# A graph network and two attention passes: start with x by columns, bias as a 129th column, and part of each chunk's chain given to ScalarE

## The chip, the cores and the metric

The kernel runs on one core of one Trainium2 chip. The metric is the device time of one execution in microseconds, the median of several runs. TensorE, VectorE, ScalarE, GpSimd and SyncE are the core's engines; the profile calls them PE, DVE, ACT, POOL and SP.

## The reference

N = 4096 rows, F = 128 columns, all in float32. `adj` is 4096 x 4096, row-normalised.

```python
h = maximum(layernorm(x), 0)
# graph layer, hyperbolic; log0(y) = arctanh(|y|) y/|y|, exp0(v) = tanh(|v|) v/|v|
g = h_add(exp0(log0(h) @ embed), embed_bias)
neigh = exp0(adj @ log0(g))
out = exp0(log0(concat(h, neigh)) @ layer)
x = x + h_add(out, layer_bias)
# h_add(a, y): xy = a.y, a2 = a.a, y2 = y.y
#   ((1 + 2 xy + y2) a + (1 - a2) y) / (1 + 2 xy + a2 y2)
h = maximum(layernorm(x), 0)
# two passes: masked softmax over the cosine of rows, times rows, leaky relu
for beta in (beta1, beta2):
    xn = h / |h|
    h = leaky(softmax(where(adj > 0, beta * xn @ xn.T, -1e9)) @ h)
x = x + h
```

## The kernel before

The work falls into three stages.

**The start.** SyncE loads x in four quarters (L323), then the first eight tiles of the transposed adjacency (L331). VectorE takes mean and variance of each of the 32 row blocks (L1191, L1195), the inverse root (`inv_sqrt`, L1127) and normalises block by block (L1204). TensorE transposes the blocks (`h_transposes`, L413), ScalarE applies relu on the way out of PSUM (L782), TensorE multiplies with `embed` (L427) and with the vector `web` = embed . bias (L433), and ScalarE takes squares and a copy of each product (`g_out`, L763). VectorE sums the squares of h itself (L1215). When all eight products are copied (`g_copied`), TensorE multiplies h with the first half of `layer` (L441), and ScalarE copies that out (`h1_out`, L772). VectorE meanwhile works through small 128x32 operations: `norm` (L1136), `product_scalars` (L1164), `norm`, `atanh_over` (L1145), with a tanh and logarithms that ScalarE does on request, and then makes v, the right side of the aggregation, block by block (L1245). TensorE does ten warm-up matmuls (L481) and waits for v's blocks.

**The aggregation.** For each of eight chunks of 512 columns (`aggregate`, L459) TensorE sums 32 float32 matmuls of 128x512 over tiles in a ring that SyncE refills as tiles are used. After the first four matmuls of chunk c+1 it does the layer product of chunk c: four transposes (L448) and four products with `w2` (L450), which need ScalarE's copy `at_sb` of the aggregated sums (L813). Two accumulators alternate. After the fourth tile it transposes the normalised rows t3 of the chunk before (L456, waits for `xn_ready`). ScalarE squares the rows for their lengths (`row_lengths`, L799). VectorE then works through the chunk's chain (`gnn_chunk`, L1267): norm of the lengths, a request for tanh (L1276), t1 = product * scale + h1 (L1283), squares (L1288), products with the layer bias `lb` (L1293), norms, arctanh, scalars, the bias scaled (L1305), the sum (L1308), x added (L1311), layer norm (L1314 to L1331), high and low float16 part into `src` (L1334, L1336) and t3 (L1342). Each engine takes its instructions strictly in the order written, and requests to ScalarE go over the semaphores `asked` and `told`, counted per chunk (`ASKS_CHUNK`). ScalarE's last work in a chunk is a copy of the new x to x_sb (L822); next it waits for the following aggregation and copies it:

```python
act.wait_ge(agg_tiles, c * NT + NT)                                   # L808
nc.scalar.activation(at_sb, acc_ps[:, parity, :], ACT.Copy).then_inc(at_ready, 1)   # L813
```

**The pairs.** The two attention passes go over pairs of 512-row chunks in 144 half steps, software-pipelined in numbered slots: scores on TensorE (L622), exponential (L990) and high halves (L1000) on ScalarE, low halves (L1647) and masks (L1655, L1665) on VectorE, transposes of mirrored blocks (L608) and the weighted sums (L648 to L675) on TensorE. The chain of chunk 7 is woven in: `last_chunk` of ScalarE (L864) and of VectorE (L1423) are the same steps cut at twelve pauses, and at each pause one slot of the pairs runs. Before its first product TensorE needs at_sb of chunk 7 (L499, ScalarE's L870), then t3 of chunk 6 (L503).

Of the kernel before, what the change touches and what calls it, by code (L numbers as in the profile page):

```python
# [26 lines left out]
def build(nc, x, adj, adj_t, embed, layer, embed_bias, layer_bias, beta1, beta2, out):  # L27
# [33 lines left out]
    WARM = 10  # L61

    ctx = ExitStack()
    with ctx:
# [17 lines left out]
        h1_sb = set1[:, NB * F:2 * NB * F].rearrange("p (b f) -> p b f", f=F)  # L82
# [19 lines left out]
        scr_a = work[:, 0:NB * F].rearrange("p (b f) -> p b f", f=F)  # L102
# [10 lines left out]
        at_sb = accs[:, :, :].rearrange("p b w -> p (b w)")[:, 0:CH]  # L113
        unused = accs[:, :, :].rearrange("p b w -> p (b w)")[:, CH:2 * CH].rearrange("p (b f) -> p b f", f=F)

        w1 = sb("w1", [F, 2 * F])
        w2 = sb("w2", [F, F])
# [22 lines left out]
        web = sb("web", [F, 1])  # L140
        ones_h = sb("ones_h", [P, P], f16)
        small = sb("small", [P, 16, NB])
        lengths = small[:, 11, NB // 2:NB // 2 + CB]
        hh = sb("hh", [P, NB])
# [11 lines left out]
        g_ps = [s_ps[:, i, 0:CH].rearrange("p (b f) -> p b f", f=F) for i in range(2)]  # L156
        h1_ps = [s_ps[:, i // 2, ts(i % 2, CH)].rearrange("p (b f) -> p b f", f=F) for i in range(4)]
        gb_ps = acc_ps[:, 0, 0:NB]
        w_ps = s_ps[:, 0, 0:CH].rearrange("p (b f) -> p b f", f=F)
        xt_ps = s_ps[:, 1, 0:CH]  # L160
        ht_ps = [acc_ps[:, 2 + i, :] for i in range(2)]
        rows_ps = s_ps[:, 0, CH:2 * CH].rearrange("p (b f) -> p b f", f=F)
        rows_last_ps = acc_ps[:, 2, :].rearrange("p (b f) -> p b f", f=F)


        w_last_ps = acc_ps[:, 3, :].rearrange("p (b f) -> p b f", f=F)
# [12 lines left out]
        x_in = [sem(f"x_in{i}") for i in range(XP)]  # L179
        embed_in = sem("embed_in")  # L180
# [9 lines left out]
        xs_ready = sem("xs_ready")  # L190
# [4 lines left out]
        gb_done = sem("gb_done")  # L195
# [8 lines left out]
        lengths_made = sem("lengths_made")  # L204
        xn_ready = [sem(f"xn_ready{i}") for i in range(2)]
# [51 lines left out]
        adj_v = adj.rearrange("(b p) j -> b p j", p=P)  # L257

# [56 lines left out]
        ASKS_CHUNK = 5  # L315
# [5 lines left out]
        def _(sp):  # L321
            for i in range(XP):
                sp.dma_start(x_sb[:, ts(i, NB // XP), :], x_v[:, ts(i, NB // XP), :]).then_inc(x_in[i], 16)  # L323
# [84 lines left out]
        def _(pe):  # L408
            pe.wait_ge(consts_made, 6)
            pe.wait_ge(embed_in, 16 * 2)  # L410


            def h_transposes(r):  # L413
                pe.wait_ge(xs_ready, r + 1)
                wait(pe, ht_copied, r - 1)
                for b in range(CB):
                    last = nc.tensor.transpose(ht_ps[r % 2][:, ts(b, P)], scr_b[:, r * CB + b, :], ident[:, :])
                last.then_inc(ht_done, 1)

            h_transposes(0)  # L420
            for r in range(NC):
                if r + 1 < NC:
                    h_transposes(r + 1)
                pe.wait_ge(ht_copied, r + 1)
                wait(pe, g_copied, r - 1)
                for b in range(CB):
                    last = nc.tensor.matmul(g_ps[r % 2][:, b, :], ht_sb[:, ts(r * CB + b, P)], w1[:, 0:F],  # L427
                                            start=True, stop=True)
                last.then_inc(g_done, 1)
                if r == 0:  # L430
                    pe.wait_ge(web_made, 1)
                for b in blocks(r):
                    last = nc.tensor.matmul(gb_ps[:, b:b + 1], ht_sb[:, ts(b, P)], web[:, :], start=True, stop=True)  # L433
                last.then_inc(gb_done, 1)
# [1377 lines left out]
```

## Time and profile before

| | us |
|---|---|
| median of three runs (lowest, highest) | 976.91 (976.67, 977.71) |
| the profiled execution | 978.14 |
| its span, first to last instruction | 976.6 |
| TensorE busy | 929.2 (95%) |
| VectorE busy | 818.8 (84%) |
| ScalarE busy | 511.2 (52%) |
| mean granted clock of TensorE | 0.989 |

A time of a row is counted from the start of the span. L numbers are lines of the kernel before. A float32 matmul stands as two records in the trace. Busy time of an engine is no proof that it sets the end; the rows further down show who waits for whom.

### The profile page before, as it was taken

The numbers are of one execution on the slowest core, as the hardware profiler recorded it, in microseconds if no ns is written. First come the engines' busy times: TensorE is split into PE (matmuls) and PEld (weight loads), VectorE is DVE, ScalarE is ACT, GpSimd is POOL, SyncE is SP. The second block draws the span as 40 slices with busy tenths as digits, with TensorE's granted clock in tenths as the row PEclk, the third lists the DMA queues.
The fourth block names the chain that finished last, engine by engine and source line by source line (L and its number), as shares of the span: only waits on it lengthen the run. The fifth ranks groups of instructions, "written<-read, shape, count | busy, mean of one in ns | idle before, by whom it ended". The sixth has DMA issues, their size and how long they took to land.

```text
span 976.6 us, 22955 instructions
## 1 busy us (share of the span) xinstructions
PE 929.2 (95%) x9012; PEld 695.3 (71%) x9012; DVE 818.8 (84%) x2110; ACT 511.2 (52%) x756; POOL 8.0 (1%) x21
## 2 busy tenths in 40 slices
PE   2989999999996999999999999999999999999996
PEld 2944444444444878888888888778888888888885
DVE  7891888888889987888989898998778887888887
ACT  1711122212126685766656667787565565656564
POOL 0000000000000000000000000000000000000000
PEclk9899999999998999999999999999999999999999
DMA  8338988888861445565465555545565655665630
GB/s 301 143 118 285 307 285 287 277 295 283 301 229 44 174 173 207 196 246 212 179 235 192 222 217 193 180 167 217 197 217 198 246 197 204 221 232 189 246 142 36
DMA packets 29971, 207.26 MB, mean 212 GB/s; under 512 B 3632, under 2 KB 4272, under 8 KB 5296
## 3 DMA queue, kind: packets, MB, share of 16 engines
q1 hardware_dynamic: 28224, 203.44, 57.6%
q0 software_dynamic: 640, 2.10, 0.5%
q8 instruction: 71, 1.16, 0.5%
q10 hardware_dynamic: 1008, 0.33, 0.1%
q14 instruction: 28, 0.23, 0.1%
HBM read 203.75 MB, written 2.10 MB: 211 GB/s over the span
## 4 chain that ended last, share of the span: by engine, by line
PE 69%; DVE 22%; issue 5%; ACT 3%; DMA 1%; DVEq 0%; POOL 0%; SPq 0%; POOLq 0%
PE s_ps L622 17%; PE s_ps L608 10%; PE acc_ps L469 6%; PE acc_ps L675 6%; PE acc_ps L671 6%; PE acc_ps L673 6%; PE acc_ps L652 5%; PE acc_ps L648 5%; PE acc_ps L650 5%; DVE small L1132 1%; DVE small L1134 1%; DVE small L1133 1%; DVE work L1647 1%; ACT work L990 1%; PE s_ps L427 1%
## 5 line engine op out<-in xcount | busy, mean ns | idle before, releaser
L990 ACT ACTIVATE work<-s_ps,beta_bias,beta_scale 128x1024 f32<-128x1024 f32 x144 | 173.4, 1204 | 217.0 <-PE s_ps L622 216.9
L469 PE MATMUL acc_ps<-ring,set 128*128 128x512 f32 x512 | 223.8, 596 | 3.2 <-DVE set L1245 3.2
L1665 DVE SCALAR_TENSOR_TENSOR h_all<-ring,s_ps 128x1024 f32<-128x1024 f32 x112 | 136.7, 1221 | 65.5 <-PE s_ps L608 64.3
L469 PEld LDWEIGHTS acc_ps<-ring,set 128*128 128x128 f32 x512 | 96.8, 191 | 120.3 <-issue 117.6
L1647 DVE TENSOR_TENSOR work<-work 128x1024 f16<-128x1024 f32 x96 | 132.5, 1380 | 5.4 <-ACT work L1000 5.4
L1000 ACT ACTIVATE work<-work 128x1024 f16<-128x1024 f32 x96 | 131.5, 1369 | 3.2 <-DVE work L1655 0.2
L1655 DVE SCALAR_TENSOR_TENSOR work<-ring,work 128x1024 f32<-128x1024 f32 x96 | 116.8, 1217 | 0.0
L622 PE MATMUL s_ps<-xt 128*128 128x512 f16 x432 | 106.4, 382 | 3.8 <-ACT work L990 3.0
L622 PE MATMUL s_ps<-set 128*128 128x512 f16 x432 | 105.0, 379 | 0.5 <-ACT work L990 0.5
L671 PE MATMUL acc_ps<-set,work 128*128 128x129 f16 x576 | 102.4, 219 | 2.7 <-DVE accs L1682 2.7
L671 PE MATMUL acc_ps<-src,work 128*128 128x129 f16 x576 | 103.5, 220 | 1.4 <-DVE work L1655 1.4
L675 PE MATMUL acc_ps<-src,work 128*128 128x129 f16 x576 | 103.9, 224 | 0.0
L673 PE MATMUL acc_ps<-src,work 128*128 128x128 f16 x576 | 103.6, 221 | 0.0
L675 PE MATMUL acc_ps<-set,work 128*128 128x129 f16 x576 | 102.7, 222 | 0.0
L673 PE MATMUL acc_ps<-set,work 128*128 128x128 f16 x576 | 102.5, 219 | 0.0
L652 PE MATMUL acc_ps<-set,h_all 128*128 128x129 f16 x448 | 79.8, 222 | 0.0
L652 PE MATMUL acc_ps<-src,h_all 128*128 128x129 f16 x448 | 79.8, 222 | 0.0
L650 PE MATMUL acc_ps<-src,h_all 128*128 128x128 f16 x448 | 79.6, 219 | 0.0
L650 PE MATMUL acc_ps<-set,h_all 128*128 128x128 f16 x448 | 79.6, 219 | 0.0
L648 PE MATMUL acc_ps<-src,h_all 128*128 128x129 f16 x448 | 79.6, 219 | 0.0
L648 PE MATMUL acc_ps<-set,h_all 128*128 128x129 f16 x448 | 79.6, 219 | 0.0
L608 PE MATMUL s_ps<-ident,work 128*128 128x128 f32 x560 | 73.6, 274 | 3.0 <-DVE work L1647 3.0
(260 smaller groups left out, 1723.2 us busy)
## 6 DMA issues: line engine op xcount, KB each, us to landing
ring<-in_adj_t SPq DMA_DIRECT2D x192, 1024.0 KB, 5.0
x_sb<-in_x SPq DMA_DIRECT2D x4, 512.0 KB, 7.2
out<-x_sb POOLq DMA_DIRECT2D x8, 256.0 KB, 2.8
w<-in_layer ACTq DMA_DIRECT2D x2, 64.0 KB, 8.1
w<-in_embed ACTq DMA_DIRECT2D x1, 64.0 KB, 4.2
eb<-in_embed_bias ACTq DMA_DIRECT2D x1, 64.0 KB, 6.9
lb<-in_layer_bias ACTq DMA_DIRECT2D x1, 64.0 KB, 7.9
beta<-in_beta ACTq DMA_DIRECT2D x2, 0.5 KB, 7.2
```

The lines of the kernel that those rows point to most:

```text
L469: last = nc.tensor.matmul(agg, v_sb[:, jb, :], ring[:, k, b, :], start=jb == 0, stop=jb == NB - 1)
L608: ins = nc.tensor.transpose(turn_ps[:, ib, ts(u, P)], words[x.n % WR][:, ds(u * CH + ib * P, P)], ident[:, :])
L622: last = nc.tensor.matmul(score_ps[:, ts(u, CH)], xt[x.la][:, p, ds(x.b * CH + (x.h * HB + u) * P, P)], xt[x.la][:, q, ds(x.a * CH, CH)], ...
L648: nc.tensor.matmul(mir_ps[:, x.h, o], w[:, WORD_HI, col], src[x.la][:, q, F:AW], start=ib == 0, stop=False)
L650: nc.tensor.matmul(mir_ps[:, x.h, ds(u * PW, F)], w[:, WORD_HI, col], src[x.la][:, q, 0:F], start=False, stop=False)
L652: last = nc.tensor.matmul(mir_ps[:, x.h, o], w[:, WORD_LO, col], src[x.la][:, q, F:AW], start=False, stop=ib == CB - 1)
L671: nc.tensor.matmul(own_ps[:, ib // 2, ds(ib % 2 * PW, PW)], w[:, WORD_HI, col], src[x.la][:, q, F:AW], start=opens, stop=False, skip_group ...
L673: nc.tensor.matmul(own_ps[:, ib // 2, ds(ib % 2 * PW, F)], w[:, WORD_HI, col], src[x.la][:, q, 0:F], start=False, stop=False, skip_group_c ...
L675: last = nc.tensor.matmul(own_ps[:, ib // 2, ds(ib % 2 * PW, PW)], w[:, WORD_LO, col], src[x.la][:, q, F:AW], start=False, stop=False, ski ...
L990: nc.scalar.activation(values[x.n % VR], score_ps, ACT.Exp, bias=beta_bias[:, x.la:x.la + 1], scale=beta_scale[:, x.la:x.la + 1]).then_inc ...
L1647: V.tensor_tensor(w[:, WORD_LO, :], values[x.n % VR], w[:, WORD_HI, :], ALU.subtract)\
L1665: V.scalar_tensor_tensor(turned[x.off % MR].rearrange("p (b j) -> p b j", b=CB), ring[:, x.mir_tile % AR, :, ds(x.h * HB * P, HB * P)], 0. ...
```

## The change

Three groups of edits.

The start: x is also passed transposed (x_t) and loaded by columns, in turns with x (each 512 KB). TensorE centres the columns by a matmul with I - 1/F and needs no normalised rows; ScalarE applies relu and also squares the result; TensorE sums the squares with a column of ones (`h_lengths`); the inverse deviations `ext` come in afterwards as scalars, and as the scale of h1 when ScalarE copies it out, block by block. `web` becomes the 129th column of w1, so L433 goes. VectorE's 32 normalisations and 32 squares go. Four early warm-up matmuls, and 30 instead of 10 before the aggregation, which wait for a semaphore `closing`. Three of the eight h1 copies stand ahead of ScalarE's tanh, four more ahead of the logarithms.

The chunk: w2 . lb and layer . lb are 129th columns of the weights, so the product with the bias comes out of TensorE and costs VectorE two operations on four elements per row. x is added while t1 is scaled, the scaled bias in a second round. The request for tanh is the norm's last step. The high part of `src` is ScalarE's, on request once t2 is scaled, and so is t3, which waits for the scale (`scaled`); both stand at the end of ScalarE's turn. The low part is made by VectorE in the next chunk, behind its request for tanh.

The last chunk: the same, with one step fewer; pauses 2 and 9 move into the middle of `inv_sqrt`. PSUM places of the products change.

```diff
@@ build @@
-    WARM = 10
+    WARM = 30
+    EARLY_WARM = 4
-        w1 = sb("w1", [F, 2 * F])
-        w2 = sb("w2", [F, F])
+        w1 = sb("w1", [F, 2 * PW])
+        web = w1[:, F:F + 1]
+        w2 = sb("w2", [F, PW])
-    ASKS_CHUNK = 5
+    ASKS_CHUNK = 6
@@ sync @@
+            x_columns(0)
             for i in range(XP):
-                sp.dma_start(x_sb[:, ts(i, NB // XP), :], x_v[:, ts(i, NB // XP), :]).then_inc(x_in[i], 16)
+                if i + 1 < XP:
+                    x_columns(i + 1)
+                x_rows(i)
@@ tensor @@
+            def h_columns(r):
+                if r % 2 == 0:
+                    pe.wait_ge(xt_in[r // 2], 16)
+                wait(pe, ht_copied, r - 2)
+                nc.tensor.matmul(ht_ps[r % 3], centre, xt_in_sb[:, ts(r, CH)], start=True, stop=True)\
+                    .then_inc(ht_done, 1)
+            def h_lengths(r):
+                pe.wait_ge(ht_squared, r + 1)
+                for b in blocks(r):
+                    last = nc.tensor.matmul(hh_ps[:, b:b + 1], sq_sb[:, ts(b, P)], ones[:, 0:1], start=True, stop=True)
+                last.then_inc(hh_done, 1)
+            h_columns(0)
+            h_columns(1)
             for r in range(NC):
+                if r + 2 < NC:
+                    h_columns(r + 2)
+                h_lengths(r)
+                if r % 2:
+                    products(r // 2)
+            for r in range(NC // 2, NC):
+                products(r)
...
+            pe.wait_ge(closing, 1)
             for _ in range(WARM):
...
             aggregate(0, 0, False, False)
+            pe.wait_ge(h1_copied, NC)
             aggregate(1, 1, True, False)
@@ scalar @@
             def h1_out(r):
...
-                nc.scalar.activation(h1_sb[:, ts(r, CB), :], h1_ps[r % 4], ACT.Copy).then_inc(h1_copied, 1)
+                for b in range(CB):
+                    q = r * CB + b
+                    last = nc.scalar.activation(h1_sb[:, q, :], part(h1_ps[r % 3], b, PW), ACT.Copy,
+                                                scale=ext[:, q:q + 1])
+                last.then_inc(h1_copied, 1)
+            h_out(0)
             for r in range(NC):
+                if r + 1 < NC:
+                    h_out(r + 1)
+                h_squares(r)
+                if r % 2:
+                    g_out(r // 2)
+            for r in range(NC // 2, NC - 1):
+                g_out(r)
             log_terms(sm(4, NB), sm(5, NB), sm(6, NB))
             g_out(NC - 1)
+            for r in range(0, 3):
+                h1_out(r)
             on(ACT.Tanh, sm(5, NB), sm(4, NB))
...
@@ scalar, gnn_chunk @@
                 on(ACT.Copy, x_sb[:, ds(c * CB, CB), :], t1[:, :, :])
+                on(ACT.Copy, src[0][:, ds(c * CB, CB), F:2 * F], t2[:, :, :], scale=FS)
+                act.wait_ge(scaled, c + 1)
+                for b in range(CB):
+                    last = nc.scalar.activation(t3[:, b, :], t2[:, b, :], ACT.Copy, scale=chunk_scale[:, b:b + 1])
+                last.then_inc(xn_ready[0], 1)
@@ vector, start @@
-            for r in range(NC):
-                for b in blocks(r):
-                    ins = V.tensor_scalar(scr_b[:, b, :], x_sb[:, b, :], mean_var[:, b, 0:1], small[:, 1, b:b + 1],
-                                          ALU.subtract, ALU.mult)
-                ins.then_inc(xs_ready, 1)
...
-            for b in range(NB):
-                ins = V.scalar_tensor_tensor(v_sb[:, b, :], scr_b[:, b, :], 0.0, scr_b[:, b, :],
-                                             ALU.max, ALU.mult, accum_out=hh[:, b:b + 1])
+            step(V.tensor_tensor(sm(3, NB), ext[:, :], ext[:, :], ALU.mult))
+            dve.wait_ge(hh_done, NC)
+            ins = V.tensor_tensor(hh[:, :], hh_ps, sm(3, NB), ALU.mult)
...
+            V.tensor_tensor(rr, xy, xy, ALU.mult).then_inc(closing, 1)
@@ vector, gnn_chunk @@
-                norm(sm(4, CB), sm(1, CB), lengths, EPS, CB)
-                ask(V.tensor_copy(sm(4, CB), sm(4, CB)))
+                norm(sm(4, CB), sm(1, CB), lengths, EPS, CB, ask)
+                if not first:
+                    dve.wait_ge(told, answers[0])
+                    low_part(c - 1)
...
+                V.tensor_tensor(in_pairs(sm(9, CB)), bias_column(w_in), in_pairs(sm(3, CB)), ALU.mult)
...
+                V.tensor_tensor(sm(9, CB), sm(9, CB), h1_sb[:, rows, F], ALU.add)
...
-                for b in range(CB):
-                    ins = V.scalar_tensor_tensor(t2[:, b, :], t1[:, b, :], 1.0, lb[:, :], ALU.mult, ALU.mult,
-                                                 accum_out=small[:, 9, b:b + 1])
-                step(ins)
...
                 for b in range(CB):
-                    ins = V.tensor_scalar(t2[:, b, :], lb[:, :], small[:, 13, b:b + 1], None, ALU.mult)
+                    ins = V.scalar_tensor_tensor(t1[:, b, :], t1[:, b, :], small[:, 12, b:b + 1],
+                                                 x_sb[:, c * CB + b, :], ALU.mult, ALU.add)
                 step(ins)
                 for b in range(CB):
-                    ins = V.scalar_tensor_tensor(t1[:, b, :], t1[:, b, :], small[:, 12, b:b + 1], t2[:, b, :],
+                    ins = V.scalar_tensor_tensor(t1[:, b, :], lb[:, :], small[:, 13, b:b + 1], t1[:, b, :],
                                                  ALU.mult, ALU.add)
-                step(ins)
-                ask(V.tensor_tensor(t1[:, :, :], x_sb[:, rows, :], t1[:, :, :], ALU.add))
+                ask(ins)
...
-                step(V.tensor_scalar(src[0][:, rows, F:2 * F], t2[:, :, :], FS, None, ALU.mult))
                 answered()
-                step(V.scalar_tensor_tensor(src[0][:, rows, 0:F], t2[:, :, :], FS, src[0][:, rows, F:2 * F],
-                                            ALU.mult, ALU.subtract))
+                ask(ins)
                 step(V.tensor_tensor(sm(0, CB), sm(0, CB), sm(1, CB), ALU.mult))
                 step(V.tensor_scalar(sm(0, CB), sm(0, CB), NORM_EPS, None, ALU.max))
                 step(V.reciprocal(sm(1, CB), sm(0, CB)))
-                for b in range(CB):
-                    ins = V.tensor_scalar(t3[:, b, :], t2[:, b, :], small[:, 1, b:b + 1], FS, ALU.mult, ALU.mult)
-                ins.then_inc(xn_ready[0], 1)
+                V.tensor_scalar(chunk_scale, sm(1, CB), FS, None, ALU.mult).then_inc(scaled, 1)
```

## Rows read from the trace of the kernel before

**Rows 1.** Windows: length, busy PE, PEld, DVE, ACT, POOL, granted clock, DMA share, GB/s

```profile
32.00:34.00 2.00, 2.00 (x21) 2.00 (x20) 1.88 (x17) 1.94 (x11) 0.00 (x0) 1.00 0.34 131
...
42.00:44.00 2.00, 2.00 (x11) 2.00 (x11) 1.71 (x9) 0.76 (x1) 0.00 (x0) 0.50 0.00 0
...
184.00:212.00 28.00, 28.00 (x79) 13.30 (x78) 24.44 (x139) 5.96 (x16) 0.00 (x0) 1.00 0.84 295
...
296.00:310.00 14.00, 7.04 (x41) 4.25 (x42) 13.01 (x47) 9.20 (x16) 0.00 (x0) 0.78 0.01 1
```

**Rows 2.** Timeline, two layer products and chain starts: start, duration, instruction

```profile
177.36 0.60 PE L448 MATMUL s_ps<-ident,accs 128*128 128x128 f32 x4
...
180.63 0.17 DVE L1139 TENSOR_SCALAR small<-small 128x4 f32<-128x4 f32 x1
...
206.59 0.60 PE L448 MATMUL s_ps<-ident,accs 128*128 128x128 f32 x4
...
210.10 0.16 DVE L1139 TENSOR_SCALAR small<-small 128x4 f32<-128x4 f32 x1
```

**Rows 3.** Timeline, VectorE, pieces of one chunk's chain

```profile
184.00 0.16 DVE L1280 TENSOR_TENSOR small<-small 128x4 f32<-128x4 f32 x1 [0.34 <-ACT small L754]
...
186.63 0.28 DVE L1293 SCALAR_TENSOR_TENSOR t<-t,lb 128x128 f32<-128x128 f32 x1
...
187.60 0.17 DVE L1296 COPY small<-small 128x4 f32<-128x4 f32 x1
...
197.72 0.87 DVE L1305 TENSOR_SCALAR t<-lb,small 128x128 f32<-128x128 f32 x4
...
198.63 1.14 DVE L1308 SCALAR_TENSOR_TENSOR t<-t,small 128x128 f32<-128x128 f32 x4
...
200.64 0.87 DVE L1314 BATCH_NORM_STATS2 stats<-t 128x6 f32<-128x128 f32 x4
...
206.34 0.87 DVE L1331 TENSOR_SCALAR t<-t,small 128x128 f32<-128x128 f32 x4
...
207.96 0.69 DVE L1336 SCALAR_TENSOR_TENSOR src<-t,src 128x512 f32 x1
```

**Rows 4.** Timeline, passage to the pairs, and ScalarE's rescaling of the last chunk

```profile
291.08 0.60 ACT L870 ACTIVATE accs<-acc_ps 128x512 f32<-128x512 f32 x1 [1.47 <-PE acc_ps L469]
...
294.83 0.25 ACT L802 ACTIVATE accs<-acc_ps 128x128 f32<-128x128 f32 x1
...
298.57 0.66 PE L456 MATMUL s_ps<-ident,t 128*128 128x128 f32 x4 [3.47 <-DVE t L1342]
...
298.58 0.17 DVE L1139 TENSOR_SCALAR small<-small 128x4 f32<-128x4 f32 x1
...
357.42 1.28 ACT L854 ACTIVATE t<-t,small 128x128 f32<-128x128 f32 x4
```

**Rows 5.** Timeline, the start; at 193.72 aggregation at full clock

```profile
5.00 1.64 DVE L1191 BATCH_NORM_STATS2 stats<-x_sb 128x6 f32<-128x128 f32 x8 [5.00 <-DMA x_sb<-in_x]
...
34.77 1.06 PE L427 MATMUL s_ps<-w,src 128*128 128x128 f32 x8
...
35.67 0.95 PE L433 MATMUL acc_ps<-web,src 128*128 128x1 f32 x8
...
41.48 1.28 ACT L754 ACT_TABLE_LOAD   x1
...
41.61 10.33 PE L441 MATMUL s_ps<-w,src 128*128 128x128 f32 x64 [1.02 <-ACT work L770]
...
45.22 0.23 ACT L754 ACTIVATE small<-small 128x32 f32<-128x32 f32 x1 [2.46 <-DVE small L1169]
...
51.77 2.40 PE L481 MATMUL acc_ps<-src,ident 128*128 128x128 f32 x20
...
57.41 14.81 PE L469 MATMUL acc_ps<-ring,set 128*128 128x512 f32 x30 [3.24 <-DVE set L1245]
...
193.72 13.04 PE L469 MATMUL acc_ps<-ring,set 128*128 128x512 f32 x30
```

More of the change, by code:

```diff
@@ L24, with build @@
 from contextlib import ExitStack
-def build(nc, x, adj, adj_t, embed, layer, embed_bias, layer_bias, beta1, beta2, out):
+def build(nc, x, x_t, adj, adj_t, embed, layer, embed_bias, layer_bias, beta1, beta2, out):
     f32, f16, b16, i32 = mybir.dt.float32, mybir.dt.float16, mybir.dt.bfloat16, mybir.dt.int32
@@ L179, in build @@
         x_in = [sem(f"x_in{i}") for i in range(XP)]
+        xt_in = [sem(f"xt_in{i}") for i in range(XP)]
         embed_in = sem("embed_in")
@@ L409, in _ @@
             pe.wait_ge(consts_made, 6)
[L410 to L415, printed above, removed]
-                for b in range(CB):
-                    last = nc.tensor.transpose(ht_ps[r % 2][:, ts(b, P)], scr_b[:, r * CB + b, :], ident[:, :])
-                last.then_inc(ht_done, 1)
-            h_transposes(0)
-            for r in range(NC):
-                if r + 1 < NC:
-                    h_transposes(r + 1)
-                pe.wait_ge(ht_copied, r + 1)
+            for _ in range(EARLY_WARM):
+                nc.tensor.matmul(acc_ps[:, 3, 0:P], ident[:, :], ident[:, :], start=True, stop=True)
@@ L432, in _ @@
-                for b in blocks(r):
-                    last = nc.tensor.matmul(gb_ps[:, b:b + 1], ht_sb[:, ts(b, P)], web[:, :], start=True, stop=True)
-                last.then_inc(gb_done, 1)
-            pe.wait_ge(weights_in, 16 * 5)
+            h_columns(0)
+            h_columns(1)
+            for r in range(NC):
+                if r + 2 < NC:
+                    h_columns(r + 2)
+                h_lengths(r)
+                if r == 1:
+                    pe.wait_ge(web_made, 1)
+                if r % 2:
+                    products(r // 2)
@@ L449, in layer_product @@
                 for b in range(CB):
-                    last = nc.tensor.matmul(w_ps[:, b, :], at_sb[:, ts(b, P)], w2[:, :], start=True, stop=True)
+                    last = nc.tensor.matmul(part(w_ps, b, PW), at_sb[:, ts(b, P)], w2[:, :], start=True, stop=True)
                 last.then_inc(w_done, 1)
@@ L1379, in chunk_stats @@
             def chunk_stats(c):
-                step(V.tensor_tensor(t1[:, :, :], x_sb[:, ds(c * CB, CB), :], t1[:, :, :], ALU.add))
                 for b in range(CB):
@@ L1429, in last_chunk @@
                 dve.wait_ge(lengths_made, c + 1)
-                norm(sm(4, CB), sm(1, CB), lengths, EPS, CB)
-                ask(V.tensor_copy(sm(4, CB), sm(4, CB)))
+                norm(sm(4, CB), sm(1, CB), lengths, EPS, CB, ask)
+                dve.wait_ge(told, answers[0])
+                low_part(c - 1)
                 pause(0)
```

197 lines of the change are left out of this document (115 added, 82 removed).

## Prediction

> **What bounds the kernel now.** The windows come first [rows 1]. While TensorE sums the adjacency tiles it is busy 28.00 of 28.00 us at full clock, and VectorE 24.44, so TensorE sets that stage's pace. From 296 to 310, between the last aggregation and the settled pair stage, TensorE is busy only 7.04 of 14.00 us: there the end waits for VectorE's chain. The timeline of one turn [rows 2] shows how close the two run: TensorE starts one chunk's layer product at 177.36 and the next at 206.59, a turn of 29.23; VectorE starts one chunk's chain at 180.63 and the next at 210.10, 29.47. TensorE never waits, because its next product needs only ScalarE's copy of the aggregated sums (at_sb), which ScalarE makes the moment an aggregation ends (291.08 for chunk 7, [rows 4]), long before VectorE has finished the chunk before. VectorE's lag costs only at the end: the last chunk's row lengths start at 294.83, VectorE takes them up at 298.58 [rows 4]. The start is a serial chain of its own, up to the first aggregation matmul at 57.41 [rows 5].
>
> **The turns.** Pieces of the chain on VectorE [rows 3]. The copy that asked for tanh goes; it is a step like L1296, 0.17 and a pitch of 0.20. The low part, 0.69 long (L1336), comes in while tanh is out, where VectorE idles 0.34 now (L1280): 0.69 - 0.34 - 0.20 = +0.15. Bias column from PSUM and its add to h1's column, two 4-element operations, with a computed address: 0.10 to 0.50, I take 0.30, the pitch of such steps being 0.08 to 0.20. The four products with the bias go, 186.63 to 187.60: -0.97. Bias scaling, sum and addition of x last 197.72 to 200.64, 2.92; two rounds like L1308 (1.14 and a step, 1.17) are 2.34, with 0.10 for the address: -0.48. At the end, 206.34 to the next chain's start at 210.10 is 3.76; there remain one small operation (0.08), the scaling (0.91), and four steps at 0.20: 1.79, so -1.97. Sum -3.0: from the chain's first step to the scale made, 29.47 - 3.0 = 26.5.
>
> So VectorE does less. But the four rescalings into t3 are now ScalarE's, behind a wait for that scale, and they are the last thing in ScalarE's turn: **the next chunk's copy into at_sb is queued behind them**, and behind that copy is TensorE's next layer product. Four such scalings of a 128x128 tile take 1.19 to the start of the next instruction (357.42, 1.28 with its tail [rows 4]). The high part, 0.6, starts when t2 is scaled and is over by the time the scale is made (four steps, 0.8): nothing, unless the scale comes earlier. Then the copy 0.60 and 0.05 to TensorE. From a product's start to the chain's is 180.63 - 177.36 = 3.27 in that turn, of which the first part is VectorE's lag; from the product's 0.6 + 1.0 and four squares of 0.25 each it is 1.55 + 1.23 = 2.78. The loop closes: 2.78 + 26.5 + 1.2 + 0.65 = 31.13 from product to product, against TensorE's own 29.23. TensorE waits 1.9 in every turn, for chunks 2 to 6. The first turn has no split and no low part (two instructions of 0.69, [rows 3] for one of them), its loop is 31.13 - 1.4 = 29.75; TensorE's first turn has no transposes either and is 0.4 shorter, 28.8: 0.9. Sum 0.9 + 5 x 1.9 = **+10.4**. What is queued behind the waiting ScalarE is that copy, then row lengths and tanh; who waits is TensorE, then VectorE. DMA is not late: the tiles are asked for by TensorE's own steps.
>
> **The passage to the pairs.** In today's times, with all later by 10.4: chunk 6's product starts at 265.05 + 10.4 = 275.4 (177.36 + 3 turns is 265.05), scale made at 275.4 + 2.78 + 26.5 = 304.7, t3 written and at_sb(7) started at 305.9, where the aggregation has been over since 301.3. Today the copy starts at 291.08 [rows 4] and the lengths 3.75 later; so at 309.6, and VectorE at 310.7 with its 1.1 of squares: 12.1 later than 298.58, of which 10.4 is told: **+1.7**. TensorE idles 3.8 before this product and may do it at half clock, which is in the 3.75 only partly (up to +0.9). In the last chunk's own chain the bias products (0.97) and 0.48 go and the copy (0.20), and the low part (0.69) and 0.2 come: **-0.8**. The pauses' shift inside norm and deviations moves the same work to other places: 0, covered by VectorE's own back-to-back order (13.01 of 14.00 [rows 1]); if a slot fell badly, one mask of 1.2.
>
> **The start.** ScalarE now does a relu and a square of 128x512, each at_sb's 0.60 and a pitch of 0.5 behind one another, and the products' four squares (0.25 each, like L802) and copy (0.5): 1.5 [rows 4], in the order h, square, g. TensorE's squares-by-ones wait for a square that stands behind g_out, and g_out waits for the products behind them. So two rows cost in series: g_out 1.5, relu and square 1.0, lengths 0.8, columns 0.87 (two records of L469 at full clock, 13.04 for 30), lengths 0.8, products 0.9 (34.77 to 35.67): 5.9. The x columns land at 5.0 as x did (VectorE's start); the first products end near 14.8 at half clock, three rounds more 31.8 (two have no columns), four g_out of 1.5, logs 0.4, the last g_out: 39.8, against 41.5 now (the table load at 41.48 follows the last copy): -1.7. The rest of VectorE's chain is as long as now, but tanh, which answers at 45.22 today, stands behind three rounds of h1 scaled block by block: 4 x 0.3 = 1.2 a round, and TensorE, idle for 2.5 before them, does them at the half clock that 42 to 44 shows after today's pause [rows 1]: twice 0.9, say 1.75 each. 39.9 + 3 x 1.75 + 1.2 + table load 1.28 = 47.7: tanh 2.5 later than today, so v 2.5 later. Bounds: at full clock 45.7, +0.5; with the first rounds slow too, up to +7; with the lengths hidden, -5.
>
> The warm-up of 30 is 60 records; 20 took 2.40, so 7.2 after `closing`, which comes 9 before v: it fits if h1 is through, else up to 2 over. It gives back what the first 30 aggregation records lose, 14.81 against 13.04 [rows 5]: -1.8. Taken together **+1.5** (2.5 - 1.8 + 0.8 for an overrun). The Trainium skill ("TensorE: Matmul & The Clock Gate", What's actually happening) has the throttled clock as the default that activity releases; by that rule the warm-up is worth its 1.8 whole; the row at 57.41, slow after 3.24 of idling, agrees. With no overrun the time would be 0.8 less, 988.9.
>
> x_t puts 2.1 MB ahead of the tiles. Today the first eight tiles are in by 33 (DMA share 0.34 in 32 to 34, [rows 1]); 5 us more at some 400 GB/s is 38, needed at 58: nothing. With a start at 35 it would show.
>
> **Sum.** 10.4 + 1.7 - 0.8 + 1.5 = +12.8. The profiled execution took 978.14 (span 976.6), so 990.9; it stands 1.2 above the median of 976.91: 989.7.
>
> **Rivals.**
> Faster: the copy is not late. It decides at a chain of 24.6 (29.23 - 2.78 - 1.2 - 0.65): if the parts save 4.9, not 3.0, TensorE keeps its 29.23 and VectorE waits for each product. Then at 295.9 instead of 298.58 it starts the last chain: -2.7, -0.8, start +1.5 to -3: 972 to 975, say 974. For: every removal is real; against: the rows add up to 3.0, and ScalarE's four scalings cannot be moved ahead of their wait. 0.15.
> The clock falls in every turn: TensorE idles 1.9 before each product. At 41 it fell after 1.02 of idling [rows 5], but before 298.57 TensorE idled 3.47 and the four transposes behind took 0.66, the 0.60 of full clock and not its double [rows 2, 4]. If it fell, the product, 1.5 long, would take 3.0 within the loop: six times 1.5, +9: 999. The Trainium skill ("TensorE: Matmul & The Clock Gate", same section) lets an idle engine fall back to the throttled clock; the trace shows both outcomes. 0.13.
> The start gives what it seems made for: products and squares overlap, tanh is not late, v at 50 to 52: -6 instead of +1.5, and the turns stay +11.3: 982. 0.12.
> It cancels: a start at -6 with half the wait per turn, 977: 0.04.
> The forecast has 0.56.
>
> **The numbers.** Faster than by 0.2% (2 us, about what this measurement can tell) needs the first rival: 0.16. Within 0.2%: 0.04. Slower: 0.80. The range leaves out the first rival and the far side of the second: 979 to 999; the unknown pieces (0.4 a turn over six turns, 2.4; start -5 to +7) lie in it.
>
> **What would show it.** Right: ScalarE's rows for t3 end just before each at_sb copy; TensorE idles about 1.9 ahead of L448's like, and product to product is 31 in five turns; VectorE idles 4.6 before each chain (lengths waited for); tanh of the start waits for h1 copies, not for VectorE. Wrong: a turn still 29.2, at_sb copied as the aggregation ends, or the first aggregation matmul before 52.

## The result and the profile after

The changed kernel took 1000.58 us (median of six runs, 996.75 to 1002.61); the kernel before, measured beside it, 977.84 (six runs, 976.67 to 980.9). The ratio is 1.0228, with a 95% interval of 1.0203 to 1.0252. So it is slower, as forecast, but by 22.7 us and not by 12.8: 1000.58 lies just beyond the forecast range of 979 to 999. The profiled run took 1001.52 with a span of 999.9, 23.3 more than the 976.6 of before.

The span splits at four events that both traces show. Each piece of before comes from the timeline of the same events as in [rows 2, 4, 5].

| piece | before | after | difference | forecast |
|---|---|---|---|---|
| start, to the first aggregation matmul | 57.41 | 69.34 | +11.9 | +3.3 |
| from there to the first layer product | 32.67 | 30.98 | -1.7 | -1.8 |
| first layer product to that of chunk 6 | 174.99 | 186.36 | +11.4 | +10.4 |
| product of chunk 6 to VectorE's last chain | 33.51 | 35.41 | +1.9 | +1.7 |
| from there to the end | 678.0 | 677.8 | -0.2 | -0.8 |

One line is far off, the first: of the 10.5 by which the forecast sum of 12.8 falls short of 23.3, 8.6 are the start's and 1.0 the turns'. In the changed kernel's numbering L444 centres the columns, L451 sums the squares (`h_lengths`), L457 makes the products, L479 those for h1, L520 is the warm-up, L507 the aggregation, L486 and L488 the layer product, L875 and L937 the copies into at_sb, L864 the row lengths, L888 t3, L1208 the first step of a norm.

Windows of after: length, busy PE, PEld, DVE, ACT, POOL, granted clock, DMA share, GB/s.

```profile
14.00:16.00 2.00, 1.13 (x5) 0.30 (x3) 1.70 (x15) 1.69 (x10) 0.00 (x0) 1.00 0.83 326
16.00:18.00 2.00, 1.01 (x7) 1.01 (x7) 1.83 (x12) 1.95 (x4) 0.00 (x0) 0.86 0.10 37
18.00:44.00 26.00, 22.26 (x82) 18.03 (x82) 9.33 (x63) 8.66 (x36) 0.00 (x0) 0.50 0.80 324
...
98.00:313.00 215.00, 204.89 (x557) 95.52 (x556) 156.21 (x914) 53.96 (x148) 0.00 (x0) 1.00 0.78 269
```

From 18 to 44 TensorE ran at 0.50, its 1.2 GHz level, all through the rounds of the new start, although it was busy 22.26 of 26.00; 32 to 34 in [rows 1] is at 1.00. In the turns, 98 to 313, the clock is 1.00 throughout, but TensorE is busy 204.89 of 215.00, where [rows 1] show 28.00 of 28.00.

The start, TensorE's timeline of after: start, duration, instruction, in brackets the idle time before it and what ended it.

```profile
13.11 1.16 PE L457 MATMUL s_ps<-w,src 128*128 128x129 f32 x8
14.11 1.02 PE L444 MATMUL acc_ps<-xt,accs 128*128 128x512 f32 x2
16.99 1.50 PE L451 MATMUL acc_ps<-ones,set 128*128 128x1 f32 x8 [1.86 <-ACT set L834]
18.36 2.05 PE L444 MATMUL acc_ps<-xt,accs 128*128 128x512 f32 x2
...
21.77 2.07 PE L457 MATMUL s_ps<-w,src 128*128 128x129 f32 x8
...
26.56 1.87 PE L451 MATMUL acc_ps<-ones,set 128*128 128x1 f32 x8 [1.02 <-ACT set L834]
...
31.70 2.07 PE L457 MATMUL s_ps<-w,src 128*128 128x129 f32 x8
...
36.50 3.57 PE L451 MATMUL acc_ps<-ones,set 128*128 128x1 f32 x16 [2.72 <-ACT set L834]
...
50.44 2.75 PE L479 MATMUL s_ps<-w,src 128*128 128x129 f32 x16 [2.21 <-ACT work L812]
...
60.74 6.86 PE L520 MATMUL acc_ps<-src,ident 128*128 128x128 f32 x60
```

This is the ping-pong that the prediction described: products (13.11) and columns (14.11), then a wait of 1.86 for a square that stands behind g_out on ScalarE. Then the same eight records that take 1.16 take 2.07, and a round of two rows, 5.9 in the forecast, is 8.7, 9.9 and 8.2 long (13.11, 21.77, 31.70, 39.93). The products for h1 begin when the last g_out is done, at 50.44; [rows 5] have them at 41.61.

VectorE and ScalarE of after, the same stretch:

```profile
40.18 0.19 DVE L1285 TENSOR_TENSOR hh<-acc_ps,small 128x32 f32<-128x32 f32 x1 [15.43 <-PE acc_ps L451]
...
56.10 1.28 ACT L796 ACT_TABLE_LOAD   x1
57.40 0.23 ACT L796 ACTIVATE small<-small 128x32 f32<-128x32 f32 x1
...
57.73 0.19 DVE L1244 TENSOR_TENSOR small<-small 128x32 f32<-128x32 f32 x1 [3.05 <-ACT small L796]
```

VectorE has nothing to do for 15.43 and then waits 3.05 for the tanh behind the h1 copies.

One turn of after (it answers to [rows 2]), all engines:

```profile
255.39 0.66 PE L486 MATMUL s_ps<-ident,accs 128*128 128x128 f32 x4 [1.83 <-ACT accs L875]
...
258.22 0.17 DVE L1208 TENSOR_SCALAR small<-small 128x4 f32<-128x4 f32 x1 [4.68 <-ACT accs L864]
...
284.87 1.28 ACT L888 ACTIVATE t<-t,small 128x128 f32<-128x128 f32 x4
...
286.05 0.57 ACT L875 ACTIVATE accs<-acc_ps 128x512 f32<-128x512 f32 x1
...
286.68 0.66 PE L486 MATMUL s_ps<-ident,accs 128*128 128x128 f32 x4 [1.83 <-ACT accs L875]
```

Read from top to bottom this is the loop: 2.83 to VectorE's chain, 26.65 to t3, 1.18 to the copy, 0.63 to TensorE, 31.29 in all. TensorE waits 1.83 for a copy of sums that were complete some 4.4 before the copy began (its product could have started at 284.85, and experiment 1 has the copy begin 3.2 before a product that does not wait), and VectorE idles 4.68 before each chain.

The layer product of chunk 7, in the passage to the pairs, from TensorE's timeline of after:

```profile
317.97 1.12 PE L486 MATMUL s_ps<-ident,accs 128*128 128x128 f32 x4 [3.97 <-ACT accs L937]
```

Here the wait is 3.97 and the four transposes take 1.12, near double the 0.60 to 0.66 of the turns.

### The profile page after: what moved, and what is told of

It is laid out like the page before. It is cut to its first block, busy times and chain, and to the rows that moved or that the text cites. A ratio compares the mean times of both kernels' runs of the same rounds, so it can differ in the third digit from the quotient of the medians.

```text
span 999.9 us, 22892 instructions
## 1 busy us (share of the span) xinstructions
PE 950.4 (95%) x9044; PEld 706.5 (71%) x9044; DVE 786.5 (79%) x1930; ACT 532.1 (53%) x823; POOL 8.0 (1%) x21
## 3 DMA queue, kind: packets, MB, share of 16 engines
q8 instruction: 71, 1.16, 0.5%
## 4 chain that ended last, share of the span: by engine, by line
PE 64%; DVE 21%; issue 5%; ACT 5%; DVEq 0%; POOL 0%; ACTq 0%; POOLq 0%
PE s_ps L663 17%; PE s_ps L649 9%; PE acc_ps L717 6%; PE acc_ps L713 6%; PE acc_ps L715 6%; PE acc_ps L694 5%; PE acc_ps L690 5%; PE acc_ps L692 5%; PE acc_ps L507 3%; DVE small L1203 1%; DVE small L1202 1%; DVE small L1201 1%; DVE work L1720 1%; ACT accs L864 1%; ACT work L1057 1%
## 5 line engine op out<-in xcount | busy, mean ns | idle before, releaser
L507 PE MATMUL acc_ps<-ring,set 128*128 128x512 f32 x512 | 222.1, 592 | 1.7 <-DVE set L1315 1.7
L507 PEld LDWEIGHTS acc_ps<-ring,set 128*128 128x128 f32 x512 | 96.2, 190 | 117.7 <-issue 115.7
```

Source lines behind the costliest of these rows:

```text
L507: last = nc.tensor.matmul(agg, v_sb[:, jb, :], ring[:, k, b, :], start=jb == 0, stop=jb == NB - 1)
```

## The experiments

All ratios are to the kernel before. It was measured anew beside each group: 977.03 (nine runs) for the first four, 978.32 (eleven) for the next four, 979.95 (seventeen) for the last two. "First aggregation matmul" is written FA.

**1. The copy first.** The changed kernel, with the next chunk's copy into at_sb ahead of the high part and t3 in ScalarE's turn, and likewise for chunk 7.

```diff
-                act.wait_ge(agg_tiles, c * NT + NT)
                 if first:
+                    act.wait_ge(agg_tiles, NT)
                     act.wait_ge(h1_copied, NC)
-                else:
-                    act.wait_ge(w_done, c)
-                nc.scalar.activation(at_sb, acc_ps[:, parity, :], ACT.Copy).then_inc(at_ready, 1)
+                    nc.scalar.activation(at_sb, acc_ps[:, parity, :], ACT.Copy).then_inc(at_ready, 1)
...
                 on(ACT.Copy, x_sb[:, ds(c * CB, CB), :], t1[:, :, :])
+                if not c_last(c):
+                    act.wait_ge(agg_tiles, c * NT + 2 * NT)
+                    act.wait_ge(w_done, c + 1)
+                    nc.scalar.activation(at_sb, acc_ps[:, 1 - parity, :], ACT.Copy).then_inc(at_ready, 1)
                 on(ACT.Copy, src[0][:, ds(c * CB, CB), F:2 * F], t2[:, :, :], scale=FS)
```

> The changed kernel with one thing moved: ScalarE copies the next chunk's aggregated sums (at_sb) before it makes the high part and t3, not behind them. No work is added or removed. Queue theory (TensorE's layer product waits for a copy that stands behind ScalarE's wait for the scale): product to product falls from 31.3 to 29.2 us, the 1.83 us waits are gone, VectorE waits some 2.7 us for each chunk's lengths, and the time falls by 11 for the turns and about 1 at the passage: 1000.6 - 12 = 988. Rival theory (the chain through VectorE and ScalarE is serial and sets the turn wherever the copy stands): turn stays at 31, time within 1 us of 1000.6.

988.01 (983.16 to 989.19), ratio 1.0086 [1.0055, 1.0118]. Timeline of this kernel:

```profile
180.93 0.60 ACT L886 ACTIVATE accs<-acc_ps 128x512 f32<-128x512 f32 x1 [3.04 <-PE acc_ps L507]
...
184.16 0.60 PE L486 MATMUL s_ps<-ident,accs 128*128 128x128 f32 x4
...
184.66 1.28 ACT L890 ACTIVATE t<-t,small 128x128 f32<-128x128 f32 x4
...
187.06 0.17 DVE L1207 TENSOR_SCALAR small<-small 128x4 f32<-128x4 f32 x1 [2.43 <-ACT accs L864]
```

The copy is made 3.2 before TensorE wants it; the product has no wait, turns are 29.24 again, and the six waits (10.1 us in sum) are gone: from the first layer product to that of chunk 6 it is 174.99, as in the kernel before. So the whole loss of the turns was the place of one ScalarE instruction, not the amount of work. VectorE now idles 2.43 in each turn, about what the change had saved it. From the product of chunk 6 (271.88) to the last chain (306.14) it is 34.26, 1.15 less than in the changed kernel. Two more pieces of this profiled run differ: FA came 3.4 earlier, by the clock in the rounds (last section), and the stretch behind the last chain was 1.8 longer, which experiment 7, with the same edit, does not show (677.7).

**2. t3 back on VectorE.** The changed kernel, L888 undone.

```diff
@@ scalar @@
-                act.wait_ge(scaled, c + 1)
-                for b in range(CB):
-                    last = nc.scalar.activation(t3[:, b, :], t2[:, b, :], ACT.Copy, scale=chunk_scale[:, b:b + 1])
-                last.then_inc(xn_ready[0], 1)
@@ vector @@
-                V.tensor_scalar(chunk_scale, sm(1, CB), FS, None, ALU.mult).then_inc(scaled, 1)
+                for b in range(CB):
+                    ins = V.tensor_scalar(t3[:, b, :], t2[:, b, :], small[:, 1, b:b + 1], FS, ALU.mult, ALU.mult)
+                ins.then_inc(xn_ready[0], 1)
```

> The changed kernel with the four rescalings into t3 back on VectorE; the high part stays ScalarE's, ahead of the copy into at_sb. Queue theory: the copy then stands behind the high part only, which ends 29.3 us behind the product (28.76 for its start in the changed kernel's trace, and 0.5): ready at 29.9 against TensorE's own 29.2. So a turn of 29.9, a wait of 0.5 to 0.7 left in each, though VectorE does 0.7 us more per chunk than in the changed kernel: 8 to 9 us faster, 992. Rival (VectorE's work sets the turn): more work on VectorE, so slower by 0.7 a turn, 1005.

989.01 (986.98 to 990.44), ratio 1.0104 [1.0068, 1.014]; turns of 29.86. It is 11.6 less than the changed kernel, more than the 8 to 9 expected: in the profiled run the turns give 8.0, the passage 2.0 and an earlier FA 1.3.

Timeline of this kernel, one layer product:

```profile
247.55 0.66 PE L486 MATMUL s_ps<-ident,accs 128*128 128x128 f32 x4 [0.39 <-ACT accs L875]
```

A wait of 0.39 to 0.41 is left in four turns (none in the first, 0.72 in the second), since the high part (0.64) still stands ahead of the copy. The turn is shorter than with t3 on ScalarE, by 1.4: work taken off VectorE cost more than it saved, because of what it was put in front of.

**3. The suspected wait, put into the kernel before.** ScalarE waits at the end of each chunk's turn until VectorE has written t3; nothing else changes.

```diff
                 on(ACT.Copy, x_sb[:, ds(c * CB, CB), :], t1[:, :, :])
+                act.wait_ge(xn_ready[0], c + 1)
```

> The kernel before, with nothing moved, but ScalarE waits at the end of each chunk's turn until VectorE has written t3, so that the copy into at_sb stands behind it as in the change. Queue theory: chain start to t3's end is 29.55 in the trace of before, and with 2.78 ahead of it and 0.70 behind a turn is 33.0 instead of 29.23: 3.0 for the first, 19 for five more, 4 at the passage to the pairs, + 26: 1004. Rival (the copy's place is harmless, TensorE has slack for it): below 980.

1010.04 (1008.68 to 1013.54), ratio 1.0337 [1.0299, 1.0375]. Timeline of this kernel, a layer product at half clock and one at full clock:

```profile
255.62 1.11 PE L448 MATMUL s_ps<-ident,accs 128*128 128x128 f32 x4 [3.65 <-ACT accs L813]
...
290.14 0.66 PE L448 MATMUL s_ps<-ident,accs 128*128 128x128 f32 x4 [2.17 <-ACT accs L813]
```

One wait in the old order costs 33 us; turns are 31.7 to 34.5. The mechanism is shown by itself. The forecast of 33.0 a turn, 1004 in all, was too low because the clock fell in four of the six turns. Behind 3.65 and 4.08 the four transposes took 1.11 and 1.12, near double. Behind 2.72 and 2.60 they still took 0.65 and 0.66, but the clock fell right after them, and from there to the transposes of t3 it is 13.4 instead of 11.7. So what the second rival of the prediction describes does occur, and the changed kernel comes close to it (see the last section).

**4. Fillers in the start.** The changed kernel, with eight matmuls of 128 columns on the identity ahead of `h_lengths(r)` for r = 2, 4, 6.

```diff
+                if r in (2, 4, 6):
+                    fill(8)
                 h_lengths(r)
```

> The changed kernel with eight filler matmuls of 128x128 (16 records, 1.9 us at full clock, 3.9 at half) in TensorE's order ahead of the sums of squares of rows 2, 4 and 6 in the start, where it idles. Clock theory (the start is late because TensorE, waiting for ScalarE in every round, falls to the 1.2 GHz clock at 17 and stays there to 45): the fillers keep the full clock, a round of two takes about 6 instead of 9.6 us, v is ready 7 to 10 us earlier: 992. Rival theory (the rounds are slow by their serial order, the clock costs little): no gain or a loss of up to 4 us, as the fillers stand in the way at the half clock.

992.78 (992.3 to 995.08), ratio 1.0154 [1.0119, 1.0189]. Windows of this kernel, and then its timeline:

```profile
14.00:32.00 18.00, 16.90 (x124) 14.41 (x123) 9.80 (x71) 10.43 (x38) 0.00 (x0) 1.00 0.87 346
```

```profile
13.26 1.16 PE L457 MATMUL s_ps<-w,src 128*128 128x129 f32 x8 [0.20 <-DVE bsq L1275]
...
19.80 1.14 PE L457 MATMUL s_ps<-w,src 128*128 128x129 f32 x8
...
26.33 1.14 PE L457 MATMUL s_ps<-w,src 128*128 128x129 f32 x8
...
60.69 1.52 PE L513 MATMUL acc_ps<-ring,set 128*128 128x512 f32 x3 [1.76 <-DVE set L1321]
```

Work was added and the time fell by 7.8. The clock is 1.00 from 14 to 32, a round is 6.5, FA is at 60.69 instead of 69.34; turns are unchanged (waits of 1.85 to 1.87). So in these two profiled runs 8.65 of the start's +11.9 is the clock in the rounds, and the dependencies alone cost what the prediction had for them (60.7).

**5. tanh ahead of the h1 copies.**

```diff
-            for r in range(0, 3):
-                h1_out(r)
             on(ACT.Tanh, sm(5, NB), sm(4, NB))
-            for r in range(3, NC - 1):
+            for r in range(NC - 1):
```

> Edit: in ScalarE's start the tanh that VectorE waits for stands ahead of all h1 copies, where the changed kernel has three rounds of them (twelve copies) in front of it. Theory 'the rounds at half clock are the loss': the last g_out stays where it was (50.2), since the rounds are untouched; tanh answers some 3 earlier (in the changed kernel VectorE waited 3.05 for it, up to 57.40), v and the first aggregation matmul 3 earlier at most, 66 to 67 instead of 69.3, the time 997 to 999. Rival 'the h1 copies ahead of tanh are the loss': the first aggregation matmul at 58 to 60, the time about 990. The turns stay at 31.3 in both.

999.15 (997.59 to 999.68), ratio 1.0203 [1.0181, 1.0224]. VectorE no longer waits for tanh. From its logarithms (47.07; 48.87 in the changed kernel) to FA (65.46; 69.34) it takes 18.4 instead of 20.5: 2.1 gained, not 3, because the warm-up, 58.76 to 65.5, now ends after v, which VectorE starts at 64.06. The rounds are nearly as slow as before (8.4, 8.4 and 8.2); what they are shorter by is the rest of the 3.9 by which FA came earlier. The rival that made this the main loss fell. In one turn of this run, after a wait of 2.34, the transposes took 0.99 and the product 1.93: the clock fell there, which cost 1.2 of what had been gained.

**6. The start one round apart.** TensorE makes the products of a row behind the lengths of the next row, ScalarE takes g_out two rows behind its squares. No instruction is added or removed.

```diff
                 h_lengths(r)
...
-                if r % 2:
-                    products(r // 2)
-            for r in range(NC // 2, NC):
-                products(r)
+                if r:
+                    products(r - 1)
+            products(NC - 1)
@@ scalar @@
-                if r % 2:
-                    g_out(r // 2)
-            for r in range(NC // 2, NC - 1):
-                g_out(r)
+                if r > 1:
+                    g_out(r - 2)
+            g_out(NC - 2)
```

> Edit: the start is pipelined one round apart: TensorE does the products of a row right behind the lengths of the next row, ScalarE takes g_out two rows behind the squares, so no engine waits for what it has just asked for. Nothing is added or taken out. Theory 'rounds at half clock': in the changed kernel TensorE idled between products and lengths, fell to half clock at 17 and a round of two rows took 9.6 to 9.9; with the dependencies one round apart it stays at full clock (or, if it falls, is still busy), a row takes 2.5 to 3, the last g_out ends at 31 to 38 instead of 50.2, the first aggregation matmul at 50 to 58 instead of 69.3, and the time falls by 11 to 19: 982 to 990. Rival 'the clock falls whatever the order, and the round's length is TensorE's own work at half clock': rounds of two of 7 to 8, g_out at 44 to 46, the time 994 to 997. The turns stay at 31.3 in both.

985.7 (985.22 to 987.78), ratio 1.0075 [1.0053, 1.0098]. Timeline of this kernel, and then its windows:

```profile
15.38 1.14 PE L457 MATMUL s_ps<-w,src 128*128 128x129 f32 x8
...
18.03 1.14 PE L457 MATMUL s_ps<-w,src 128*128 128x129 f32 x8
...
20.67 1.14 PE L457 MATMUL s_ps<-w,src 128*128 128x129 f32 x8
...
53.56 6.67 PE L506 MATMUL acc_ps<-ring,set 128*128 128x512 f32 x15 [1.75 <-DVE set L1313]
```

```profile
10.00:26.00 16.00, 15.85 (x109) 13.27 (x110) 12.64 (x91) 14.21 (x59) 0.00 (x0) 0.99 0.87 329
26.00:32.00 6.00, 6.00 (x30) 6.00 (x29) 2.60 (x15) 3.46 (x20) 0.00 (x0) 0.50 1.01 427
```

A row takes 2.65, which is as long as ScalarE's squares, g_out and relu in a row (2.64) and as TensorE's three groups (2.65): both engines are full. TensorE is busy 15.85 of 16.00, and FA is at 53.56: 15.8 earlier than in the changed kernel, 3.9 earlier than before. The new start is worth something once no engine waits for what it has just asked for.

**7. All three moves** (1, 5 and 6 together).

> Edit: the changed kernel with three moves together: the next chunk's copy into at_sb ahead of the high part and t3 in ScalarE's turn; the tanh of the start ahead of the h1 copies; the start pipelined one round apart. Theory: each takes its own stretch, so the gains add: turns of 29.2 without waits (about 12 less), first aggregation matmul at 47 to 55 instead of 69.3: 967 to 977, below both the kernel before and the changed one. Rival 'VectorE is the bound of the turns once they follow one another closely' : turns 29.5 to 30, 3 more. Rival 'the tiles are late when the start is short' : TensorE idles behind the first aggregation matmuls, the start gains less than 14.

971.45 (971.25 to 976.27), ratio 0.9935 [0.9914, 0.9956]. TensorE's timeline of this kernel, at FA:

```profile
45.16 6.86 PE L519 MATMUL acc_ps<-src,ident 128*128 128x128 f32 x60
51.86 8.32 PE L506 MATMUL acc_ps<-ring,set 128*128 128x512 f32 x19
```

FA is at 51.86, the product of chunk 6 at 257.75, the last chain at 292.03, the span 969.7. The gains add: 17.5 in the start, 11.4 in the turns, 1.1 in the passage, from 999.9. Turns are 29.24 with no wait, and the tiles are not late: no matmul of the aggregation waits for one. It is 0.65% faster than the kernel before, with an interval clear of 1. Both rivals fell.

**8. And the last chunk's lengths earlier.** As 7, with ScalarE's lengths ahead of the first slot of the pairs.

```diff
-                pause(-1)
                 row_lengths(c)
+                pause(-1)
```

> Edit: as the kernel with the three moves, and in the last chunk ScalarE takes the row lengths straight behind its copies, ahead of the first slot of the pairs instead of behind it. Theory: the lengths come some 2.4 earlier, VectorE starts the last chunk's chain up to that much earlier, and the time is 1 to 2.4 less than with the three moves alone. Rival: that slot of the pairs is needed as early as the lengths, and the time is the same within 0.5.

970.81 (969.99 to 973.64), ratio 0.9921 [0.9903, 0.9939]. The median is 0.64 below that of 7, between the 0.5 of the rival and the 1 of the theory, and the two intervals overlap: at most a small gain. The timelines of the passage, of 7 and then of 8:

```profile
288.38 1.19 ACT L1052 ACTIVATE work<-s_ps,beta_bias,beta_scale 128x1024 f32<-128x1024 f32 x1
...
292.03 0.17 DVE L1203 TENSOR_SCALAR small<-small 128x4 f32<-128x4 f32 x1 [4.86 <-ACT accs L860]
```

```profile
289.87 1.21 ACT L1052 ACTIVATE work<-s_ps,beta_bias,beta_scale 128x1024 f32<-128x1024 f32 x1
290.09 0.17 DVE L1203 TENSOR_SCALAR small<-small 128x4 f32<-128x4 f32 x1 [2.43 <-ACT accs L860]
...
291.13 2.74 PE L662 MATMUL s_ps<-xt 128*128 128x512 f16 x6 [4.32 <-ACT work L1052]
```

VectorE starts 1.94 earlier, and the exponential for which TensorE waits comes 1.49 later; the spans are 969.6 and 969.7. (The product of chunk 6 is 0.46 later in 8; counted from it, the chain starts 2.40 earlier and the exponential comes 1.03 later.) So most of what the lengths gain is lost in the slot of the pairs, which is needed nearly as early.

**9 and 10. The warm-up by itself**, in both directions.

```diff
@@ changed kernel @@
-    WARM = 30
+    WARM = 10
@@ kernel before @@
-    WARM = 10
+    WARM = 24
```

> Edit: the changed kernel with 10 warm-up matmuls ahead of the aggregation instead of 30. Theory 'the warm-up gives back what the first aggregation matmuls lose' (the prediction put it at 1.8): the warm-up ends 4.5 earlier, at about 63, TensorE idles some 6 before the first aggregation matmul, which does not move; the first 30 records take 14.5 to 15 instead of 13.2, and the time is 1.6 to 2 more: 1002 to 1003. Rival 'the clock is held up by the layer products in front of it anyway': the first records as fast, the time the same within 0.5.

> Edit: the kernel before with 24 warm-up matmuls ahead of the aggregation instead of 10, and nothing else: this part of the change alone. Theory: 48 records of 0.115 end at 51.77 + 5.6 = 57.4, just as v is there; the first 30 aggregation records take 13.1 instead of 14.8, and the time falls by 1.7, to 975.5. Rival 'it costs its own length': the warm-up overruns v, and the time is the same or up to 0.5 more.

With 10, from FA to the first layer product it is 32.38 (64.92 to 97.30) instead of 30.98: +1.4. The time, 1000.59 (998.13 to 1003.01), ratio 1.0218 [1.0192, 1.0243], is that of the changed kernel and does not show it; the forecast of 1002 to 1003 missed. An effect of 1.4 is smaller than what varies without it: in this profiled run FA came 4.4 earlier and the stretch behind the last chain was 1.8 longer. With 24 in the kernel before, the same piece is 30.98 (59.39 to 90.37) instead of 32.67: -1.7. The 1.8 of the prediction was right to 0.1 for this piece. The time, 978.09 (976.2 to 981.84), ratio 0.9979 [0.9964, 0.9994], is 1.9 less than the 979.95 beside it, just clear of the noise. The profiled run by itself shows no gain (span 977.0 for 976.6), since FA came 2.0 later in it: the clock rose later in the old start, where four transposes at 28.23 took 1.09 and those at 27.78 in the kernel before 0.63.

## Why the prediction was right or wrong

**The turns: right.** The four terms of the loop were 2.78, 26.5, 1.2 and 0.65; the trace has 2.83, 26.65, 1.18 and 0.63. The sum of 31.13 is 31.29, a wait of 1.9 is 1.83 (2.30 in the second turn), and +10.4 is +11.4: the first turn grew by 0.65 for 0.9, the second by 2.52 and the other four by 2.05 each for 1.9. Experiments 1 to 3 show the cause from three sides: the copy moved out, t3 moved back, the wait put into the old kernel.

**The passage: right** in size, +1.9 for 1.7; TensorE waits 3.97 for 3.8 there and does the transposes near half clock, as the prediction allowed. **The last chunk: small and unsure,** -0.2 for -0.8; nothing was tried on it.

**The warm-up: right,** -1.7 for -1.8, shown for its piece of the span by 9 (+1.4 without it) and 10 (-1.7 with it). The overrun of 0.8 did not occur in the changed kernel, where TensorE idles 1.74 before FA; it occurs as soon as tanh comes earlier (5 and 7).

**The start: wrong.** The term that failed is the round of "5.9": g_out 1.5, relu and square 1.0, lengths 0.8, columns 0.87, lengths 0.8, products 0.9. It was made of rows at full clock, and with it the last g_out was to end at 39.8; it ended at about 50.2. The dependencies were as told, and the fillers, which leave them and hold the clock, give FA at 60.69 against the 60.7 that the forecast adds up to. (Two errors cancel in that: a round at full clock is 6.5, not 5.9, and what follows the last g_out is 19.1, not 20.9.) What was missing is TensorE's clock: behind the first wait of such a round (1.86, at 16.99) it fell to its 1.2 GHz level and was there from 18 to 44, which made every piece of TensorE's in the loop longer, and the rounds 8.2 to 9.9. With the waits filled (experiment 4) or taken out by order (experiment 6) it stayed at full clock from 14 to 32, or to about 26. The prediction applied that doubt to the turns, as a rival with a chance of 0.13, and not to the start, where it stood as one end of the bounds ("with the first rounds slow too, up to +7"). Even that end fell short: it was meant for tanh and v, and tanh came 12.2 later (57.40 for 45.22), FA, which waits for v, 11.9.

The Trainium skill ("TensorE: Matmul & The Clock Gate", A second HAM failure mode: psum-queue depth-cycling) tells of a kernel in which TensorE idles so often between short groups that the clock swings. The rows agree in part: waits of 1.86, 1.02 and 2.72 between groups of matmuls, and 0.50 from 18 to 44; but in this profile the clock did not swing, it stayed down between the waits too. In experiments 5 and 9, with the same rounds, it did rise once between them and fell again (below).

Of the rivals, "the copy is not late" fell with the first wait at L486. "The clock falls in every turn" fell for this change: the transposes behind four waits of 1.83 took 0.66 each time, and so did those behind 2.30. In single turns of the same kernel it is not excluded, as the last section shows. "The start gives what it seems made for" is what experiment 6 shows to be possible, with another order of the same instructions.

## What to carry to other kernels

Before moving work from a busy engine to an idle one, write down what stands behind it in the idle engine's queue and who needs that: here four scalings of 1.2 us on a half-idle engine held back a copy whose sums had been complete for some 4 us, and the copy ahead of them gave back all that the turns had lost. A chain in which two engines hand each other one piece at a time paid twice here, once in waiting and once in TensorE's clock; shift the producer by a round, so that each engine works on what was asked for a round ago. And price such a chain at both clock levels before choosing one.

## What the runs showed of the hardware beyond that

The clock's fall is not a fixed property of the code. In the changed kernel the lengths at 16.99 took 1.50 behind an idle time of 1.86, as shown above. The same instructions in experiments 1 and 9, whose starts are the same up to there, TensorE's timelines in that order:

```profile
16.83 1.05 PE L451 MATMUL acc_ps<-ones,set 128*128 128x1 f32 x8 [1.86 <-ACT set L834]
...
23.36 1.64 PE L451 MATMUL acc_ps<-ones,set 128*128 128x1 f32 x8 [1.87 <-ACT set L834]
```

```profile
17.08 1.05 PE L451 MATMUL acc_ps<-ones,set 128*128 128x1 f32 x8 [1.87 <-ACT set L834]
...
19.75 1.87 PE L457 MATMUL s_ps<-w,src 128*128 128x129 f32 x8
...
24.35 1.05 PE L451 MATMUL acc_ps<-ones,set 128*128 128x1 f32 x8 [1.02 <-ACT set L834]
```

In the three it fell first at 17, at about 23.5 and at about 20 (in the last it rose again and fell again), and FA came at 69.34, 65.91 and 64.92. In experiment 5 it fell at about 18, rose at about 24 and fell again at about 28. That one start so varies by 4.4 us, which could account for most of the spread of the changed kernel's times (996.75 to 1002.61); one profiled run of a kernel with such a start is a poor measure of it. So the 8.65 of experiment 4 rests on the latest FA among these profiled runs; the medians, 1000.58 and 992.78, differ by 7.8.

Nor does the length of a wait decide it. One turn of experiment 9 and the passage of experiment 10, TensorE's timelines:

```profile
158.59 0.66 PE L486 MATMUL s_ps<-ident,accs 128*128 128x128 f32 x4 [2.34 <-ACT accs L875]
...
171.98 0.60 PE L494 MATMUL s_ps<-ident,t 128*128 128x128 f32 x4
```

```profile
298.89 1.11 PE L456 MATMUL s_ps<-ident,t 128*128 128x128 f32 x4 [3.50 <-DVE t L1342]
```

In the turns waits of 1.83 to 1.88 did not make the clock fall, nor did 2.30 in the changed kernel and 2.34 in experiment 6. Behind 2.34 in experiments 5 and 9 it fell: in the first the transposes took 0.99, in the second it fell right after them, and the 11.7 to the transposes of t3 became 13.4. Behind 2.60 and 2.72 in experiment 3 it fell too. And 3.47 of idling before t3's transposes in the kernel before left them at 0.66, where 3.50 in experiment 10 gave 1.11.

In experiment 6 it fell at 26, where TensorE had been busy for 15.85 of 16.00 us; in experiment 7, with the same order, it was 1.00 from 18 to 30; in experiment 8, again the same, it fell at about 28. In experiment 4 it fell at about 33, among matmuls that had not waited since 30.20. So a wait is not needed for a fall; experiment 4 makes it likely that the waits caused the one at 17, but does not prove it. In the old start, 1.02 of idling before the products for h1 left the clock at 0.50 from 42 to 44, and 1.03 in experiment 10 left it at 1.00 from 42 to 50. The Trainium skill ("TensorE: Matmul & The Clock Gate", What's actually happening) has the clock follow how busy TensorE has been of late, and says that one and the same kernel may meet the switch at different points; the second half agrees with the rows above, the first does not explain the fall at 26 by the busy column. Why it fell there stays open.
